# Layer 2 of a four-layer image kernel: GpSimd weighs a unit's state ahead of making the next drive, and keeps its drives four units ahead

## The reference

```python
dA = exp(dt_l[..., None] * A)
h = h * dA + (dt_l * u_l)[..., None] * B_l[:, :, None, :]
y = einsum('bkdn,bkn->bkd', h, C_l)
```

## Time and profile before

| | us |
|---|---|
| median of 3 runs | 36854.54 |
| lowest and highest run | 36848.28, 36859.58 |
| the profiled execution | 36884.56 |
| its span | 36882.7 |
| DVE busy | 31959.7 (87%) |
| PE busy | 31182.5 (85%) |
| POOL busy | 28596.0 (78%) |
| ACT busy | 24679.3 (67%) |

### The profile page before, as it was taken

The page is one execution under the profiler, slowest core; times in us unless marked ns, Lnnn a source line. Parts: engine busy times, 40 slices in busy tenths (PEclk is TensorE's granted clock), DMA queues, the critical chain, the costliest instruction groups (busy, mean ns, idle before and its releaser), DMA issues. The chain is left out here.

```text
span 36882.7 us, 298078 instructions
## 1 busy us (share of the span) xinstructions
PE 31182.5 (85%) x69732; PEld 12933.9 (35%) x69732; DVE 31959.7 (87%) x22739; ACT 24679.3 (67%) x46805; POOL 28596.0 (78%) x13244
## 2 busy tenths in 40 slices
PE   8888888888888888888888888888888888888888
PEld 3333333333333333333333333333333333333333
DVE  8969889698896988969889798896988969889698
ACT  6757667576675766757667576675766757667576
POOL 6949869498694986949869497694976949769497
PEclk9999999999999999999999999999999999999999
DMA  3424434244342443424434244342433424434244
GB/s 118 164 96 163 143 115 164 95 164 143 117 164 96 164 143 116 163 95 164 143 116 164 97 164 142 117 164 95 164 140 119 164 95 164 141 119 163 96 164 140
DMA packets 1387462, 5030.81 MB, mean 136 GB/s; under 512 B 164272, under 2 KB 165816, under 8 KB 1381440
## 3 DMA queue, kind: packets, MB, share of 16 engines
q1 hardware_dynamic: 1385536, 5010.20, 39.1%
HBM read 4938.25 MB, written 71.30 MB: 136 GB/s over the span
## 5 line engine op out<-in xcount | busy, mean ns | idle before, releaser
L712 PE MATMUL PS<-WORK,CST 128*128 128x512 f32 x37568 | 18564.5, 641 | 3435.7 <-POOL WORK L612 1542.5
L601 POOL TENSOR_TENSOR WORK<-WORK,XN 128x1024 f32<-128x1024 f32 x7024 | 16408.1, 2363 | 252.3 <-ACT BIG L1157 252.3
L712 PEld LDWEIGHTS PS<-WORK,CST 128*128 128x128 f32 x37568 | 7456.4, 204 | 14479.7 <-issue 11148.6
L1157 ACT ACTIVATE PS<-WORK,AN 128x512 f32<-128x512 f32 x17408 | 11314.4, 680 | 936.3 <-DVE WORK L1779 200.4
L1772 DVE TENSOR_TENSOR_SCAN PS<-PS,HST,WORK 128x1024 f32<-128x1024 f32 x4224 | 9905.0, 2345 | 171.8 <-ACT PS L1157 160.8
L1772 DVE TENSOR_TENSOR_SCAN WORK<-PS,HST,WORK 128x1024 f32<-128x1024 f32 x1920 | 4497.6, 2343 | 30.8 <-ACT PS L1157 30.8
L1157 ACT ACTIVATE WORK<-HST,WORK,AT 128x1 f32<-128x1 f32 x6144 | 2329.4, 379 | 1864.6 <-POOL WORK L601 1824.6
L1779 DVE TENSOR_TENSOR WORK<-PS,WORK 128x1024 f32<-128x1024 f32 x2624 | 3214.0, 1225 | 90.5
L682 POOL MEMSET XN<- 128x66 f32 x32 | 4.9, 153 | 4018.5 <-DVE SM L1650 3833.9
L612 POOL TENSOR_TENSOR WORK<-WORK,CWIDE 128x1024 f32<-128x1024 f32 x1296 | 3063.0, 2363 | 13.3 <-DVE WORK L1772 13.3
L712 PE MATMUL PS<-QLAST,CST 128*128 128x512 f32 x4672 | 2523.5, 667 | 580.7 <-POOL QLAST L612 307.7
(11 more groups left out here) (186 smaller groups left out, 34655.9 us busy)
## 6 DMA issues: line engine op xcount, KB each, us to landing
XN<-xbc_rows SPq DMA_DIRECT2D x4096, 512.0 KB, 3.7
WORK<-xbc_rows SPq DMA_DIRECT2D x2816, 512.0 KB, 4.4
CWIDE<-xbc_rows SPq DMA_DIRECT2D x2304, 512.0 KB, 3.8
BIG<-in_spec_dram SPq DMA_DIRECT2D x32, 2048.0 KB, 12.0
X<-in_x_dram SPq DMA_DIRECT2D x68, 512.0 KB, 4.2
xbc_rows<-L0S SPq DMA_DIRECT2D x512, 64.0 KB, 3.4
out_dram<-X SPq DMA_DIRECT2D x64, 512.0 KB, 4.0
xbc_rows<-WORK SPq DMA_DIRECT2D x128, 32.0 KB, 1.6
```

What stands on the lines that cost most here:

```text
L601: nc.gpsimd.tensor_tensor(S.both(S.Q[u % 7]), S.both(S.DU[u // SN % 2]), S.wide(S.BW, u).unsqueeze(1).to_broadcast([P, 2, NT]), MUL).then_ ...
L712: return nc.tensor.matmul(o, w, r, start=start, stop=stop)
L1157: return nc.scalar.activation(o, i, f, **k)
```

## The change

POOL makes four drives ahead of its loop instead of three. In the loop, for each unit u, the weighing of u now stands before the drive, and the drive is that of u + 4. The place of `make_du` in the loop stays. Nothing else is edited.

```diff
                 make_du(0)
                 e.wait_ge(dw_act, NCH)
-                for u in range(3):
+                for u in range(4):
                     make_drive(u)
                 for u in range(S.units):
                     g, n = u // SN, u % SN
                     if g + 1 < KDIR * NCH and n == 12:
                         make_du(g + 1)
-                    if u + 3 < S.units:
-                        make_drive(u + 3)
                     if S.on_pool(u):
                         weigh(u)
+                    if u + 4 < S.units:
+                        make_drive(u + 4)
```

## The result

| | before | changed |
|---|---|---|
| median (16 runs each), us | 36865.54 | 36930.03 |
| lowest and highest, us | 36840.6, 36907.0 | 36905.37, 36950.7 |
| profiled execution, us | 36884.56 | 36905.37 |
| its span, us | 36882.7 | 36903.5 |
| DVE busy, us | 31959.7 | 31950.9 |

The ratio is 1.0019, with a 95% interval of 1.0012 to 1.0026. The forecast was 36854, range 36804 to 36904; the medians lie 64.5 us apart. The period of a chunk, from one DU to the next, is the better measure, since it repeats.

The account below looks back on a forecast made before the run. POOL's work per chunk plus its half-microsecond stall ahead of W10 was taken as the bound. Terms of 0 for order, POOL, ACT and DVE left the profiled 36884.6 us; put on the median, 36854 us, range 36804 to 36904.

Parts of the forecast that it names:

- The two lists: POOL's order before and after, written out: no drive or weighing changes place against another; only DU and D15 swap; cost 0.
- For this D15 must not wait in its new place: POOL, D15 issued ahead of DU, 2.3 us earlier (2.8 in odd directions): claimed to find its waits met, 0 us.
- its three conditions: D15's needs: row B already loaded for D14, its buffer's state 8 summed by PE, and the present chunk's DU.
- D16 starts where it did: POOL, the drive behind the swapped DU and D15: claimed to start at 438.08 as before, so POOL loses 0 us.
- 0.54 x 496 = 268 us: Upper bound on POOL's loss, had each D15 waited as W10 does.
- one tenth of a microsecond in each of 496 places: Small waits the swap might shift, below what the timeline lists: 50 us either way, which set the range.
- POOL's period as the bound: POOL's work per chunk plus its stall ahead of W10 is the chunk period: 50.88 + 0.54 = 51.42 against 51.39.
- Its sum for the stall: PE's start to W10 takes 7.4 us; three drives of 2.363 us fill 7.1; the rest is the half microsecond idle.
- Who gets D15 earlier, who gets DU later: ACT's seam 15 loses its 1.38 us wait, without gain for DVE; `prepare` meets DU about 0.3 us after its end; 0.
- the bound of 197 us: Most that DVE could gain from an earlier D15: its waits for ACT's decays, less those at scan starts.
- The late DU: Slower rival: ACT's `prepare` waits for DU and delays seam 16 and DVE's scan 16; 258 us, 37112 us, chance 0.03.
- the cover named against it: Seam 16 waits for D16, and unit 16's decays for DVE's weighing of 14, covering a DU later by another 1.5 us.

Follow-up runs that it names:

- the added waits inside and outside the stall: Kernel before plus POOL waits for the instruction just ahead: three at D11 to D13 (inside), 36964.14 us; four at states 2, 3, 4, 6 (outside), 37261.59 us.
- the carry first: ACT's first copy of dt at state 10 moved behind that turn's seam and carry: on the kernel before 36582.8 us, on the changed kernel 36614.24 us.

## Why the prediction was wrong, point by point

- *The two lists.* Right. Drives and weighings keep their order; only DU moves, one place, 496 times.
- *"For this D15 must not wait in its new place"* and its three conditions. Right: D15 follows D14 without a gap.
- *"D16 starts where it did"*, and with it "POOL stalls nowhere new: 0 us". This is the step that failed. I went through the waits of the instruction that moved and not through those of the one that got a new neighbour. D16 waits for DU. It starts 2.44 us after DU and not 2.31. The runs show this 0.13 us a chunk in place of the 0 (61 us by the steps, and 16 to 29 in more long chunks), and nothing once that wait is taken away.
- *The bound "0.54 x 496 = 268 us".* It would have held the loss, but was tied to D15. The range was taken from "one tenth of a microsecond in each of 496 places", with the centre at 0; the true size, 0.13, was just past it. The median of before also came out 11 us higher over 16 runs than over three; without that drift the result would still lie outside, 64.5 us against 50.
- *POOL's period as the bound* (work plus the 0.53 us at W10). Right, and the reason why 0.13 us counts in full: the added waits inside and outside the stall, and the carry first, show it. Its sum for the stall does not close, though: 7.4 less 7.1 us leaves 0.3, not the half microsecond. In the trace of before the three drives run from 421.33 to 428.29, 6.96 us and not 3 x 2.363, since each starts some 0.04 us before the one ahead ends, and they begin 0.10 us before PE's 421.43: 7.40 is 6.86 and 0.54. It is this small overlap of neighbours, left out of the sum, that D16 lost.
- *Who gets D15 earlier, who gets DU later.* Right. ACT in the changed kernel, seam 15, `prepare`, seam 16:

```profile
491.62 0.38 ACT L1157 ACTIVATE WORK<-HST,WORK,AT 128x1 f32<-128x1 f32 x1
493.23 0.29 ACT L1157 ACTIVATE AT<-AN,WORK 128x16 f32<-128x16 f32 x1
495.53 0.39 ACT L1157 ACTIVATE QLAST<-HST,QLAST,AT 128x1 f32<-128x1 f32 x1 [1.77 <-POOL QLAST L601]
```

The 1.38 us of the earlier trace rows at seam 15 are gone, `prepare` starts 0.16 us after DU's end and waits for nothing, and seam 16 waits 1.77 us instead of 0.17. In 67 of the 448 chunks that have this part `prepare` does wait, by 0.4 us, as short as the prediction allowed, and the run without D16's wait shows that this costs nothing. DVE's waits for decays grew by 29 us in the group of the earlier trace rows and by 96 over all tiles (the bound of 197 us took that group alone; over all tiles it is 228). They are back where they were once the own wait is gone, so they follow from it.
- *The late DU* as the slower rival: not what happened, and the cover named against it held. Its mirror, a late D14, does cost, as the run with DU ahead of both shows.
- *The sign for "wrong"*: "if the period of a chunk differed by over 0.1 us" was met (0.13 and 0.14 by the medians over all chunks); idle time at line 601 inside the scan too, 32.6 and 6.3 us of it.

## What to carry to other kernels

When an instruction moves, list the waits of its new neighbours as well as its own. On POOL, where it is full, a dependence between two adjacent instructions was a cost even though the order alone never left it idle; put one independent instruction between producer and consumer. Read start-to-start steps, since a gap of 0.08 us carries no idle mark and still adds up over 496 places.

## What the runs showed of the hardware

- On POOL two independent 128x1024 instructions start 2.31 us apart while each is shown as 2.36 long. If the second waits for the first, the step is 2.44 us when that wait is written first of three, and 2.52 or 2.53 when it is last. A wait for the one two ahead leaves it at 2.31.
- The Trainium skill, GPSIMD Engine Reference, section "2.1 Instruction dispatch", says that completion gates what waits on an instruction's semaphore and does not hold back the next Pool instruction. This case agrees, and gives the price of being such a waiter: 0.13 to 0.21 us.
- That the order in which waits are written changes the step by 0.08 to 0.10 us was unexpected. Two pairs of kernels show it; the cause was not tried.
